# The products with V in one burst, their PSUM bank in the common ring, and a third of the low halves on GpSimd

## The reference

```python
x = x + attn(layernorm(x))        # 16 heads of 8 channels, causal softmax over 512 keys
x = x + ffn(layernorm(x))
# ffn: gates = sigmoid(x @ Wg + bg), kept where > 0.5
h = relu(einsum('td,edh->eth', x, W1) + b1[:, None, :])      # 8 experts, 512 hidden
expert_out = einsum('eth,ehd->etd', h, W2) + b2[:, None, :]
combined = einsum('te,etd->td', gates, expert_out)
```

## Time and profile before

| | |
|---|---|
| median of 3 runs | 751.51 us (751.17 to 754.06) |
| profiled execution, its own time | 752.44 us |
| span of its instructions | 750.7 us |
| TensorE busy | 714.4 us, 95% of the span |
| TensorE weight loads | 459.5 us |
| VectorE, ScalarE, GpSimd busy | 501.9, 424.2, 293.2 us |
| mean granted TensorE clock | 0.96 |

### The profile page before, as it was taken

The page is one execution under the profiler, slowest core; times in us unless marked ns, Lnnn a source line. Parts: engine busy times, 40 slices in busy tenths (PEclk is TensorE's granted clock), DMA queues, the critical chain, the costliest instruction groups (busy, mean ns, idle before and its releaser), DMA issues.

```text
span 750.7 us, 13207 instructions
## 1 busy us (share of the span) xinstructions
PE 714.4 (95%) x4515; PEld 459.5 (61%) x4515; DVE 501.9 (67%) x997; ACT 424.2 (57%) x777; POOL 293.2 (39%) x377
## 2 busy tenths in 40 slices
PE   3779999999999999999999999999999999999996
PEld 2344455667666766667566765667666766667774
DVE  7985658768766677667766777667765776536443
ACT  1444545566655665566566565666656566654442
POOL 5251223345334533344334443344334444344343
PEclk9956869999999999999999999999999999999999
DMA  6701112221131112220132111310131102100310
GB/s 178 200 2 41 30 24 71 78 54 33 23 109 52 45 31 67 80 50 17 38 95 52 39 37 49 89 48 13 29 103 52 38 3 73 30 29 2 98 29 14
DMA packets 28673, 40.23 MB, mean 54 GB/s; under 512 B 3936, under 2 KB 12648, under 8 KB 28608
## 3 DMA queue, kind: packets, MB, share of 16 engines
q1 hardware_dynamic: 28080, 39.20, 19.2%
q10 hardware_dynamic: 528, 0.20, 0.2%
HBM read 23.52 MB, written 2.23 MB: 34 GB/s over the span
## 4 chain that ended last, share of the span: by engine, by line
PE 89%; DVE 5%; issue 3%; POOL 1%; ACT 1%; DMA 0%; POOLq 0%; DVEq 0%
PE ring L1097 12%; PE pv_bank L1173 11%; PE y_bank L1217 9%; PE ring L1038 9%; PE ring L1040 8%; PE ring L1039 8%; PE y_bank L1221 8%; PE y_bank L1219 8%; PE ring L1109 6%; PE ring L1044 4%; PE ring L1159 2%; PE ring L1148 1%; PE ring L1188 1%; PE y_bank L1097 1%; DVE f_buf L1014 1%
## 5 line engine op out<-in xcount | busy, mean ns | idle before, releaser
L805 ACT ACTIVATE h_hi<-ring 128x512 fp32r<-128x512 f32 x256 | 153.4, 599 | 178.9 <-PE ring L1040 152.7
L773 ACT ACTIVATE pt<-ring 128x512 f32<-128x512 f32 x314 | 172.5, 598 | 68.3 <-PE ring L1097 67.4
L1001 DVE SCALAR_TENSOR_TENSOR h_lo<-ring,h_hi 128x512 fp32r<-128x512 f32 x192 | 131.5, 685 | 74.5 <-ACT h_hi L805 72.5
L951 DVE TENSOR_REDUCE negmax<-ring 128x1 f32<-128x512 f32 (+1 forms) x184 | 121.3, 683 | 69.2 <-PE ring L1109 69.1
L699 POOL TENSOR_TENSOR h_lo<-h_all,h_hi 128x512 fp32r<-128x512 f32 x64 | 82.2, 1285 | 161.8 <-ACT h_all L811 148.6
L1097 PE MATMUL ring<-stack 32*128 32x256 f32 (+3 forms) x994 | 120.3, 380 | 12.9 <-ACT pt L773 3.0
L692 POOL TENSOR_SCALAR_AFFINE_SELECT pt<-pt 128x512 f32<-128x512 f32 x128 | 80.1, 639 | 120.6 <-ACT pt L773 120.0
L1097 PEld LDWEIGHTS ring<-stack 32*128 32x128 f32 x994 | 65.5, 193 | 91.2 <-issue 80.5
L1217 PE MATMUL y_bank<-h_hi,w_lo 128*128 128x512 f32 x256 | 114.6, 447 | 3.8 <-POOL h_lo L699 1.6
L1038 PE MATMUL ring<-x2T_lo,w_hi 128*128 128x512 f32 x256 | 109.4, 427 | 0.0
L709 POOL TENSOR_TENSOR f_buf<-f_buf 128x512 f32<-128x512 f32 x56 | 72.3, 1292 | 85.3 <-DVE f_buf L1014 85.2
(11 more groups left out here) (129 smaller groups left out, 760.7 us busy)
## 6 DMA issues: line engine op xcount, KB each, us to landing
f_buf<-gates SPq DMA_DIRECT2D x64, 256.0 KB, 3.3
stack<-parts SPq DMA_DIRECT2D x96, 128.0 KB
x_in<-in_L_attn_x SPq DMA_DIRECT2D x8, 256.0 KB, 2.8
pt<-in_L_ffn_W SPq DMA_DIRECT2D x1, 2048.0 KB, 9.9
out_x<-f_buf SPq DMA_DIRECT2D x8, 256.0 KB, 2.3
stack<-stack SPq DMA_DIRECT2D x32, 16.0 KB
stack<-nmT SPq DMA_DIRECT2D x32, 16.0 KB
wqkv_in<-in_L_attn_w_qkv ACTq DMA_DIRECT2D x1, 192.0 KB, 3.0
```

Of the source, the lines that this page charges most:

```text
L773: sc.activation(pt[:, slot, :], b[:], ACT.Exp, scale=SCALE).then_inc(free_sem("ex", i, g, u), 1)
L805: sc.activation(h_hi[:, (i * SLOTS + s) % 3, :], bank_of("z", i, s)[:], ACT.Relu).then_inc(s_hhi, 1)
L951: v.tensor_reduce(dst, src, AX.X, ALU.max, negate=True).then_inc(free_sem("max", i, g, u), 1)
L1001: v.scalar_tensor_tensor(out=h_lo[:, (i * SLOTS + s) % 3, :], in0=bank_of("z", i, s)[:], scalar=0.0, in1=h_hi[:, (i * SLOTS + s) % 3, :].b ...
```

## The change

The three `pv` items of a group become one, which runs key blocks 0, 1, 2, 3 in a row and waits for all four causal masks of the group. Its sum goes to a bank of the ring, freed by `og`. With `pv_bank` gone `RING` is 7 (eight banks early on). `exp` 4 waits for the whole burst of the group before; the separate waits of `exp` 8 and of the chunks go. `pick_pe` starts a burst only if a bank is free, and puts it ahead of a score step only if more than two are. `POOL_SPLITS` goes from every fourth slot (8 of 32: 3, 7, ... 31) to every third (10 of 32: 2, 5, ... 29).

```diff
-RING = 6
+RING = 7
...
-POOL_SPLITS = [s for s in range(SLOTS) if s % 4 == 3]
+POOL_SPLITS = [s for s in range(SLOTS) if s % 3 == 2]
...
-                freed = ("pv", *ago[2], 0) if u < 4 else ("pv", *ago[1], 1 if u < 8 else 2)
+                freed = ("pv", *ago[2 if u < 4 else 1])
...
-                put("pe", ("pv", i, g, c), at + .5, (916, 916, 458)[c],
-                    ("pool", ("causal", i, g, c)),
-                    ("act", ("og", *ago[1])) if c == 0 else ("pe", ("pv", i, g, c - 1)),
-                    ("dve", ("v", i)))
-            put("act", ("og", i, g), at + .6, 600, ("pe", ("pv", i, g, 2)), ("pe", ("oT", *ago[2])))
+            put("pe", ("pv", i, g), at + .5, 2290, *[("pool", ("causal", i, g, c)) for c in range(3)],
+                ("pe", ("oT", *ago[2])), ("dve", ("v", i)))
+            put("act", ("og", i, g), at + .6, 600, ("pe", ("pv", i, g)), ("pe", ("oT", *ago[2])))
...
             if item[0] == "pv":
-                if pv is None or due < pv[0]:
+                if free and (pv is None or due < pv[0]):
                     pv = (due, key)
...
-                if pv and form == "full":
+                if pv and form == "full" and free > 2:
                     start(now, "pe", pv[1])
...
-                    if u == 0:
-                        wait(act, s_pv, 3 * (n - 2) + 1)
-                        slot = 4 * (g % 2)
-                    elif u == 4:
-                        if i == 0 and g == 0:
-                            act.wait_ge(*full("w1", EXPERTS - 1))
-                        wait(act, s_pv, 3 * (n - 1) + 2)
-                    elif u == 8:
-                        wait(act, s_pv, 3 * (n - 1) + 3)
+                    if u == 0 and n >= 2:
+                        act.wait_ge(*full("pv", *divmod(n - 2, GROUPS)))
+                    elif u == 4 and n >= 1:
+                        act.wait_ge(*full("pv", *divmod(n - 1, GROUPS)))
...
-                    pe.wait_ge(s_causal, 4 * n + (1, 3, 4)[c])
-                    if c == 0:
-                        wait(pe, s_og, n)
-                        pe.wait_ge(*emptied("v", i))
-                    for kb in ((0,), (1, 3), (2,))[c]:
+                    g = w[2]
+                    pe.wait_ge(s_causal, 4 * (i * GROUPS + g + 1))
+                    pe.wait_ge(*emptied("v", i))
+                    for kb in range(TB):
```

More of the change, by code:

```diff
@@ L127, in work_items @@
             put("dve", (qk + "lo", i), t0 - 14.8 + n, 750, ("act", (qk, i)))
-        put("pe", ("v", i), t0 + 12, 900, ("act", ("xT", i)), ("pe", ("pv", i - 1, GROUPS - 1, 2)))
+        put("pe", ("v", i), t0 + 12, 900, ("act", ("xT", i)), ("pe", ("pv", i - 1, GROUPS - 1)))
         put("dve", ("v", i), t0 + 12.1, 700, ("pe", ("v", i)), ("dve", ("vset", None)))
@@ L227, in emptied_by @@
         return "dve", (kind + "lo", item[1])
+    if kind == "pv":
+        return "act", ("og", *item[1:])
     if kind == "z":
@@ L273, in start @@
             form = new
-            if item[0] not in ("y", "pv"):
+            if item[0] != "y":
                 fill(item)
@@ L461, in block_program @@
         ring = [bank(f"ring{n}") for n in range(RING)]
-        pv_bank = bank("pv_bank")
         y_bank = bank("y_bank")
@@ L499, in block_program @@
         s_causal = sem("s_causal")
-        s_pv = sem("s_pv")
-        s_og = sem("s_og")
         s_rden = sem("s_rden")
@@ L777, in _ @@
                     n = i * GROUPS + g
-                    act.wait_ge(s_pv, 3 * n + 3)
+                    act.wait_ge(*full("pv", i, g))
                     if n >= 2:
                         act.wait_ge(*full("oT", (n - 2) // GROUPS, (n - 2) % GROUPS))
-                    sc.activation(o_grp[:, g % 2, :], pv_bank[:], ACT.Copy).then_inc(s_og, 1)
+                    sc.activation(o_grp[:, g % 2, :], bank_of("pv", i, g)[:],
+                                  ACT.Copy).then_inc(free_sem("pv", i, g), 1)
                 elif kind == "OT":
@@ L926, in _ @@
                     b = bank_of("v", i)
-                    wait(dve, s_pv, 3 * GROUPS * i)
+                    if i:
+                        dve.wait_ge(*full("pv", i - 1, GROUPS - 1))
                     if i == 0:
@@ L1117, in _ @@
                     continue
-                if kind not in ("y", "pv"):
+                if kind != "y":
                     b = next_bank(*w)
@@ L1161, in _ @@
                 elif kind == "pv":
-                    g, c = w[2], w[3]
-                    n = i * GROUPS + g
-                    pe.wait_ge(s_causal, 4 * n + (1, 3, 4)[c])
-                    if c == 0:
-                        wait(pe, s_og, n)
-                        pe.wait_ge(*emptied("v", i))
-                    for kb in ((0,), (1, 3), (2,))[c]:
+                    g = w[2]
+                    pe.wait_ge(s_causal, 4 * (i * GROUPS + g + 1))
+                    pe.wait_ge(*emptied("v", i))
+                    for kb in range(TB):
                         for j in range(GH):
@@ L1172, in _ @@
                             col = {0: 0, 1: 0, 3: 3 * P, 2: 2 * P * (j // 2)}[kb]
[L1173 to L1176, removed]
+                            last = mm(b[32 * j:32 * j + 32, kb * P:], v_sb[:, kb, g * GH + j, :],
+                                      pt[:, slot, col:col + T - kb * P],
+                                      start=(kb == 0), stop=(kb == TB - 1), skip_group_check=True)
+                    last.then_inc(done, 1)
                 elif kind == "oT":
                     g = w[2]
-                    pe.wait_ge(s_og, i * GROUPS + g + 1)
+                    pe.wait_ge(*emptied("pv", i, g))
                     four_transposes(b, lambda t: o_grp[:, g % 2, t * P:(t + 1) * P],
```

## The result

The changed kernel takes **729.98 us** (median of 4 runs, 729.25 to 732.47) against 751.41 (4 runs): 21.4 us less, a ratio of 0.971, 95% interval 0.968 to 0.975. I had said 736.5, range 729 to 747, and for the forecast itself 730 to 743; the measured time stands at the lower edge of both. The profiled execution was the longest of the four, 732.47 us with a span of 730.7, so its sum is 20.0 us short of before, not 21.4.

What follows compares the result with a forecast made beforehand. TensorE, busy 95% of the span, was taken as the bound. Steps -14.8, end -1.2 and waits +1.0 gave -15.0 us: 737.4 from the profiled 752.4, or 736.5 against the median 751.5; range 729 to 747.

Steps and rivals of the forecast that it cites:

- TensorE's steps: TensorE's order of steps: fewer fixed parts and changes of form, a sum of -14.8 us.
- Three chunks in one: pv products on TensorE: two of three fixed parts per group go, 64 x 0.10 = 6.4 us less; burst 2.36 us.
- The rival that the fixed parts stay: Inside a burst: TensorE drains between key blocks anyway, so merging chunks gives nothing, 743 us; 3 in 100.
- All other terms: TensorE's changes of form and score steps: -3.0, -4.3, +0.8, -1.7 and -0.2 us.
- all changes of form: TensorE's array mode changes, 664 to 556: by the skill's drain figure 108 x 0.05 = 5.8 us would go.
- The ring: PSUM ring banks: the burst holds one, a seventh comes in return; 0 us, gain excluded where TensorE has no waits.
- Waits in the middle: Cover between a group's last ex step and its burst gets a little thinner: +1 us in all, at worst 15.
- The slower rival: Each burst waits for all four masks, everything behind it too; at 0.7 us a burst +22, 759 us; 3 in 100.
- The end: Last y no longer waits for GpSimd's low half of slot 31: -1.2 us, at least 0.6.
- The start: Up to 115 us: chain of loads, exponentials and maxima kept; 0 us, +-5 for the clock.
- The clock rival: Steady part: three to eight more half-clock stretches give 5 to 14 us, 742 to 751; 6 in 100.
- activity lifting the clock: Clock grant: reduced clock is the default and activity lifts it; trace said to agree in the start and at 369 us.

Runs made afterwards that it cites:

- e5: Kernel before with six planner constants changed, so only the order moves; work, banks and splits as before: 738.91 us against 753.75, ratio 0.978.
- e2: Kernel before with the three pv chunks as one burst in its own bank, six ring banks, every fourth slot on GpSimd: 742.33 us, ratio 0.982.
- e3: Changed kernel with POOL_SPLITS as before (every fourth slot on GpSimd), burst and seventh ring bank kept: 735.11 us, ratio 0.975.
- e6: Changed kernel with other planner constants (EXP_LAG 11, FFN_LAG 56, SWITCH_DUE 0, HALF_DUE 4, other step costs): 721.22 us, ratio 0.957.
- e11: Changed kernel with planner constants FFN_LAG 50, SWITCH_DUE 0.6, PV_DUE 0.8, HALF_DUE 1: 725.15 us, ratio 0.962.
- e8: Changed kernel, its planner placing bursts after the last exponentials instead of the masks, with the program's waits kept: 734.69 us, ratio 0.974.
- e1: Kernel before with only POOL_SPLITS changed, every third slot's low half on GpSimd instead of every fourth: 748.95 us against 752.52, ratio 0.994.
- e10: Changed kernel with every second slot's low half on GpSimd (16 of 32, last slot included) instead of every third: 729.42 us, ratio 0.967.
- e12: Changed kernel with every second low half on GpSimd (last slot on VectorE) and new planner constants (EXP_LAG 10, FFN_LAG 53 and others): 721.55 us, ratio 0.957.
- e9: Changed kernel run again unchanged, as base on the chip of two later runs: 729.88 us, ratio 0.969.
- e7: Changed kernel, max and ex pairs sharing a score step only if in different halves of the array: 743.93 us, ratio 0.985.
- e4: Changed kernel with RING 6 instead of 7, the burst sharing the six banks: 743.69 us, ratio 0.987.

## Why the prediction was right, point by point

**TensorE's steps, -14.8 in the sum, -17.2 with the burst as the trace has it.** The mechanism stood and one size was off: *Three chunks in one* was put at 64 x 0.10 = 6.4 us, with 9.6 as the far side. A burst takes 2.29 us and not 2.36, so it saves 32 x 0.275 = 8.8. The fixed part of a chunk is near 0.14, as the comparison of chunks 0 and 2 in the prediction had it (0.15), not the 0.09 that I took from other changes of form. I had two rows for the same number and chose the one that was further from the thing itself, and passed over the 2290 that the change's own planner has for a burst. The rival that the fixed parts stay is out. All other terms, 8.4 us in the sum, are 8.4 when every step is priced, with the same counts and prices, so this checks the adding and not the prices. e5 tests the rule without burst or bank: 14.8 us measured for 15.5 of prices, 11 to 13 between runs at like clock. The Trainium skill (TensorE: Matmul & The Clock Gate, steps of a matmul) gave, by my estimate, 5.8 us for all changes of form (108 x 0.053; with the 0.05 that I wrote it is 5.4); the trace does not agree, with 8.8 us for the 64 fixed parts inside the products alone. What it says of the cause (TensorEngine Tiling, Tiling Modes: a change of mode drains the engine) fits the rows, but no run here separates a drain from other fixed costs.

**"The ring ... 0 us, a gain being excluded where TensorE has no waits": this step failed.** e2 and e3 differ by the seventh bank (and the place of the burst) at nearly equal step prices, and by 7.2 us in time. Two orders of one price were 3.9 us apart (e6 and e11), so a single pair is weak, but the means over thirteen kernels say some 6 us as well. By medians from several chips the change is: burst 10.2, bank 7.2, third edit 5.1, together 22.5, where the result is 21.4. By runs at like clock (0.964 to 0.966) it is 7.7, 7.7 and 3.5. More than half of the bank's gain lies in the start (5.6 of 9.7 us in the two profiles), where TensorE does wait, and for which I had put 0. How much of that is the bank and how much the clock in those executions stays open.

**Waits in the middle, +1: the sum hid more.** At their prices the steps of the middle fell by 17.6 us, its length by 16.7. That looks like the +1, but the clock gave back some 3.4 us there, so all else rose by 4.3; TensorE's idle time is 1.2 of that (3.82 to 5.05), for the rest I have no row. That the figure came near was luck. That the cover of a burst is thin was right: where e8 makes it thinner, 6.0 us of waits appear at eight bursts. The slower rival (0.5 us at each of 32) would have needed far worse.

**The end, -1.2, measured -1.8** from the last sequence's first `z` to its last transposes (53.3 to 51.5). It is the third edit's: e1 has it alone and takes 51.5, e3 lacks it and takes 53.3. 1.3 of it are left at the span's end. **The third edit**, which I had valued by its last slot alone, brings 3.6 us on the kernel before (the clock has a part in that) and 5.1 on e3; the prices account for 0.6 and 4.4 of that. e10 and e12 show less idle time of TensorE with more low halves on GpSimd, in two orders; e12's middle is also cheaper than e6's in steps. Why is open: ScalarE's second copy frees the bank earlier than VectorE's turn might, but no run separates that from VectorE's load.

**The start, 0 +-5, measured -2.0** in the profiled execution and -4.2 in e9, the same kernel. **The clock rival** was wrong in its sign: neither of the changed kernel's profiles has a stretch at half clock between 115 us and the last sequence, where before had two. Runs of before at a mean clock of 0.964 took 751.15 to 751.38 us, the one of the changed kernel at 0.964 took 732.47, so at like clock the change gives 19 us, and some 2 of the 21.4 go with the clock. Whether the new order causes that is not shown. The prediction says that the trace agrees with activity lifting the clock, in the start too. There it goes too far: from 89.3 to 106.4 us TensorE had no idle time and stayed at 0.50.

In all: the direction and the main mechanism were right. The time came 6.5 us under the forecast through a burst 2.4 us cheaper than summed, a bank put at nothing and a clock that turned out kinder, against waits that were put too low. It lies 1 us inside the range, and no rival of mine stood on that side: there the range was luck.

## What to carry to other kernels

On a TensorE that hardly waits, time still hides between steps: price each kind of step from start to start, for each form of the array before and behind it, and add up the order. For a change of planner constants alone that sum foretold 15.5 us, where 14.8 came, 11 to 13 at like clock. Over the thirteen kernels here the time less the sum stayed between 66 and 78 us, so it ranks orders only when they are far apart. Before an edit to a scheduled kernel is judged, ask how much of its gain is a better roll of the order: e5 got over half of this change's gain (11 to 13 of 19 us at like clock, 14.8 of 21.4 by medians) with no edit to the work at all. And before a bank more is put at nothing because TensorE looks busy, look at the stages one by one: here the start had 20 to 24 us of idle time, and even the middle had waits to lose.

## What the runs showed of the hardware

- Fixed costs are stable to the nanosecond: the last twelve bursts of the changed kernel, from 430 us on, take 2.290 or 2.291 us at full clock, whatever stands before or behind them.
- In the start nearly the same work (544 to 567 matmuls) takes 96.8 us (e8) to 107.7 us (e2) from first transpose to first `x2T`, with 27.3 us of it at half clock in e8 and 54.6 in e1 (107.0 us). The shortest start had the least of it. Whether the clock made it short, or the order that kept TensorE busy did both, these runs don't tell.
- Stretches at half clock also came in the busy middle. In e7 at 458.2 us,

```profile
458.20:461.60 3.40, 3.40 (x12) 2.00 (x14) 0.83 (x2) 1.09 (x2) 0.47 (x1) 0.50 0.53 121
```

TensorE has no idle time and loses 1.7 us by estimate. But 1.2 us earlier, at 457.0, it had waited 0.77 us among score steps. Before's two stretches stand behind such waits too (0.73 and 0.72 us, less than 2 us earlier), and so do those of e4 (0.81), of e7 at 120.3 (0.51) and of e8 (0.84). Such a wait is not enough: e2 waited 0.84 us at 202.6 and at 286.0, e8 1.39 us at 160.4, and no stretch followed. What else it takes is open.
